# Eight chained sub-layers for four batches on one core: a new service order for each engine's interleaved streams of steps

## The reference, cut to what matters

```python
x = x + tanh(g_xattn[l]) * XATTN[l](layernorm(x), ctx, fside)
x = x + tanh(g_ffn[l])   * FFN[l](layernorm(x))
# 0: XATTN state-space scan over 256 positions (16 states, conv4, softplus, silu gate)
#    FFN   8 experts, top 2, width 176, and a shared expert of width 352
# 1: XATTN two int8 "smooth quant" linears;  FFN ternary SwiGLU, width 1024
# 2: XATTN 16 heads with rms-normalised q, k against ctx; FFN BitNet (int8 rows, ternary weights)
# 3: XATTN one head against ctx;             FFN group-ternary SwiGLU with rms norm
```

## Time and profile before

| | |
|---|---|
| median of 3 runs | 1079.76 us (1079.28 to 1082.18) |
| the profiled execution's own time | 1082.69 us |
| its span, first to last instruction | 1080.9 us |
| mean granted clock of TensorE, of full speed | 0.89 |
| busy: TensorE, VectorE, ScalarE, GpSimd | 856.8, 737.9, 531.3, 274.2 us |

### The profile page before, as it was taken

The page is one execution under the profiler, slowest core; times in us unless marked ns, Lnnn a source line. Parts: engine busy times, 40 slices in busy tenths (PEclk is TensorE's granted clock), DMA queues, the critical chain, the costliest instruction groups (busy, mean ns, idle before and its releaser), DMA issues.

```text
span 1080.9 us, 13019 instructions
## 1 busy us (share of the span) xinstructions
PE 856.8 (79%) x4024; PEld 630.9 (58%) x4024; DVE 737.9 (68%) x1800; ACT 531.3 (49%) x1250; POOL 274.2 (25%) x362
## 2 busy tenths in 40 slices
PE   3365599865899887997987899989998689798465
PEld 1121366544678666665776676669866558476244
DVE  4799967784456997887669888854587743354632
ACT  7654643422563554665533555753454445464313
POOL 1200131102133114431642143406100514100205
PEclk9666689987999999897999999989999989699557
DMA  7622455523433202330542133206211324110002
GB/s 260 196 97 80 134 158 175 167 85 84 133 114 118 59 20 60 103 126 15 141 137 64 50 93 109 63 13 191 85 44 50 88 59 119 43 39 21 15 0 69
DMA packets 46627, 99.39 MB, mean 92 GB/s; under 512 B 4952, under 2 KB 16608, under 8 KB 45408
## 3 DMA queue, kind: packets, MB, share of 16 engines
q1 hardware_dynamic: 37344, 73.40, 21.8%
q0 software_dynamic: 9216, 25.17, 8.4%
HBM read 89.12 MB, written 9.44 MB: 91 GB/s over the span
## 4 chain that ended last, share of the span: by engine, by line
PE 37%; DVE 31%; issue 15%; POOL 9%; ACT 6%; SPq 1%; DMA 0%; POOLq 0%; DVEq 0%; ACTq 0%
PE bk L1260 24%; PE bk L1334 5%; DVE ssm_u L1866 4%; PE bk L1572 2%; DVE ssm_u L1860 2%; PE bk L1541 2%; POOL arA L846 2%; DVE lnbuf L1771 1%; DVE mx L2084 1%; ACT arB L1145 1%; POOL lnbuf L800 1%; DVE arB L2097 1%; POOL aclA L866 1%; PE bk L1684 1%; PE bk L1327 1%
## 5 line engine op out<-in xcount | busy, mean ns | idle before, releaser
L1260 PE MATMUL bk<-hTA,ringT 128*128 128x256 f32 x448 | 115.4, 405 | 1.5 <-DMA ringT<-in_w 0.8
L800 POOL TENSOR_TENSOR lnbuf<-lnbuf,mhalf 128x2 f32<-128x2 f32 x32 | 26.2, 818 | 356.0 <-DVE lnbuf L1777 356.0
L1260 PEld LDWEIGHTS bk<-hTA,ringT 128*128 128x128 f32 x448 | 89.9, 205 | 18.4 <-issue 2.1
L1145 ACT ACTIVATE arB<-bk,nb,rqs 128x256 f32<-128x256 f32 x128 | 70.9, 560 | 30.9 <-DVE nb L2087 30.7
L1866 DVE TENSOR_TENSOR_SCAN ssm_u<-ssm_da,ssm_u 128x512 f32<-128x512 f32 x64 | 81.0, 1265 | 4.7 <-DVE ssm_u L1860 0.5
L1260 PE MATMUL bk<-qk 128*128 128x256 f32 x288 | 79.6, 403 | 5.3 <-ACT arB L1145 2.9
L1260 PE MATMUL bk<-arB,cx 128*128 128x256 f32 x256 | 70.8, 400 | 9.4 <-DVE qk L2132 8.3
L1896 DVE SCALAR_TENSOR_TENSOR t1A<-thA,bk 128x256 f32<-128x256 f32 x88 | 36.6, 416 | 53.9 <-ACT thA L1070 53.5
L1185 ACT ACTIVATE arB<-bk 128x512 f32<-128x512 f32 x64 | 38.2, 596 | 61.9 <-PE bk L1541 61.7
L1334 PE MATMUL bk<-ringM,arB 128*128 128x256 f32 x256 | 66.6, 382 | 1.4 <-ACT arB L1194 1.4
L1063 ACT ACTIVATE ssm_da<-sdl,nega 128x255 f32<-128x255 f32 x128 | 57.0, 501 | 20.5 <-DVE ssm_u L1866 20.0
(11 more groups left out here) (333 smaller groups left out, 2212.9 us busy)
## 6 DMA issues: line engine op xcount, KB each, us to landing
ringT<-in_w SPq DMA_DIRECT2D x56, 384.0 KB, 3.1
ringQ<-in_wqk SPq DMA_DIRECT2D x40, 384.0 KB, 3.1
ring<-q3s POOLq DMA_DIRECT2D x32, 384.0 KB, 3.5
ring<-q7s POOLq DMA_DIRECT2D x32, 384.0 KB, 3.6
ringM<-m4s SPq DMA_DIRECT2D x32, 256.0 KB, 2.6
q3s<-qk SPq DMA_DIRECT2D x4, 512.0 KB, 7.6
q7s<-qk SPq DMA_DIRECT2D x4, 512.0 KB, 4.0
qk<-in_wo SPq DMA_DIRECT2D x4, 512.0 KB, 4.3
```

Of the source, the lines that this page charges most:

```text
L800: g.tensor_tensor(lnr, lnv, mhalf[:, 0:2], ALU.pow).then_inc(*sig(f"{k}.pool", "lnr"))
L1145: s.activation(pm[:, t, :], bank[:, t * S:t * S + S], ACT.Exp, bias=nb4[:, n, t:t + 1], scale=scale(t), accum_out=den4[:, n, t:t + 1]).the ...
L1260: return t_.matmul(dst, lhsT, rhs, start=start, stop=stop)
```

## The change

Only the numbers of `PLAN` change, for all five streams and all parts; some knots are added or dropped. Every step, operation, tile, DMA, wait and signal is the same. What differs is the order in which each engine comes to them. A few of the lines (the tables of the scan states, chunks, heads and rings change in the same way and are left out):

```diff
             "pe": {
-                "group": {0: ((0.15, 586.51), (0.9, 588.82), (2.4, 592.73), (16.15, 614.12), (18.4, 639.13), (32.15, 718.06), (34.4, 768.37),)},
...
-                "h1": {0: ((2.5, 639.64), (4.5, 680.25), (11.5, 798.78),),
...
-                "kp": {0: ((0, 1100.60), (1.5, 1100.61), (2, 1182.86), (3, 1240.57), (4, 1243.48), (5, 1261.89), (6, 1261.90), (6.5, 1263.46), (8.5, 1264.57),)},
...
-                "vo": {0: ((0, 902.41), (1, 902.72), (2, 973.33), (3, 1014.14), (4, 1066.80), (5, 1066.91), (7, 1082.33),)},
...
+                "group": {0: ((0.15, 463.90), (0.9, 463.91), (1.65, 487.73), (2.4, 542.94), (16.15, 700.84), (16.9, 705.75), (17.65, 721.62), (18.4, 722.23), (32.15, 781.82), (32.9, 781.83), (34.4, 783.04),)},
...
+                "h1": {0: ((2.5, 269.52), (11.5, 594.89),),
...
+                "kp": {0: ((0, 1016.60), (1, 1019.71), (1.5, 1020.12), (2, 1191.76), (2.5, 1191.77), (3, 1195.20), (3.5, 1197.41), (4, 1198.00), (5.5, 1202.06), (6.5, 1212.15), (7.5, 1213.26), (8.5, 1213.27),)},
...
+                "vo": {0: ((0, 829.01), (1, 868.45), (2, 876.92), (4, 898.67), (5, 902.38), (6, 997.23), (7, 1014.44),)},
...
             "dve": {
-                "group": {0: ((0.15, 584.93), (4.5, 588.79), (7.5, 626.91), (10.5, 627.22), (16.15, 633.37), (18.4, 639.42), (20.5, 656.13), (22, 658.14), (25, 702.58), (32.15, 773.64), (32.9, 773.65), (33.65, 775.66), (36.5, 776.94), (38, 828.97), (42.5, 831.18),)},
...
-                "h1": {0: ((0, 201.52), (2, 635.65), (5.5, 735.99), (8.5, 752.60), (9.5, 761.71), (10.5, 761.72),),
...
+                "group": {0: ((0.15, 464.31), (1.65, 467.22), (2.4, 535.90), (4.5, 536.21), (6, 542.49), (7.5, 542.50), (10.5, 548.39), (16.15, 722.32), (16.9, 722.33), (17.65, 725.91), (20.5, 729.60), (22, 729.81), (23.5, 731.92), (26.5, 762.23), (32.9, 787.86), (33.65, 804.98), (34.4, 806.97), (36.5, 809.29), (38, 813.75), (42.5, 822.96),)},
...
+                "h1": {0: ((0, 547.11), (9.5, 560.80), (10.5, 601.95),),
...
             "sp": {
-                "vo": {0: ((-1, 708.60), (1, 890.90), (3, 927.60), (5, 1068.37), (8, 1094.36), (9, 1096.46),)},
...
+                "vo": {0: ((-1, 837.07), (1, 868.97), (3, 890.81), (5, 894.42), (8, 1105.43), (9, 1225.71),)},
...
```

More of the change, by code:

```diff
@@ new lines, in build @@
+                "h1": {0: ((2.5, 269.52), (11.5, 594.89),),
+                    1: ((2.5, 1211.73), (11.5, 1214.26),),
+                    2: ((2.5, 2020.45), (11.5, 2030.93),),
+                    3: ((2.5, 2263.97), (4.5, 2264.92), (11.5, 2283.91),)},
+                "head": {0: ((-0.25, 1450.52), (0, 1464.23), (0.39, 1464.24), (1, 1471.53), (1.25, 1472.74), (1.39, 1477.47), (1.64, 1484.95), (2.42, 1484.96), (2.64, 1527.97), (3, 1646.90), (3.42, 1657.83), (3.64, 1657.84), (4.42, 1658.85), (4.64, 1663.75), (5, 1663.76), (5.25, 1667.20), (6, 1671.14), (6.42, 1672.72), (6.64, 1673.58), (7.39, 1675.07), (7.64, 1677.86), (8, 1677.87), (9.42, 1683.81), (9.64, 1690.67), (11.39, 1695.96), (11.64, 1710.97), (12, 1712.38), (12.25, 1712.69), (13.42, 1728.70), (13.64, 1742.59), (14.42, 1742.60), (14.64, 1748.27), (15.42, 1749.65), (17.42, 1777.19),),
[40 rows of a table added]
@@ new lines, in build @@
+                "state": {0: ((-1.2, 203.13), (-0.2, 251.04), (0.8, 311.45), (1.8, 317.33), (3.95, 325.34), (4.8, 359.44), (5.95, 359.75), (6.8, 411.02), (8.95, 432.43), (9.8, 434.44), (13.95, 466.73), (14.95, 537.86), (15.95, 546.57), (16, 546.58),),
[3 rows of a table added]
+                "ternary": {0: ((0.4, 17.54), (1.4, 173.05), (2.4, 215.17), (3.4, 316.22), (4.4, 358.85), (5.4, 413.81),)},
+                "vo": {0: ((0, 829.01), (1, 868.45), (2, 876.92), (4, 898.67), (5, 902.38), (6, 997.23), (7, 1014.44),)},
@@ L405, in build @@
-                "head": {0: ((-0.14, 1824.78), (0.25, 1827.29), (0.44, 1829.99), (1.25, 1832.63), (1.44, 1838.47), (1.81, 1838.48), (2.25, 1843.60), (2.44, 1843.61), (2.81, 1847.26), (3.25, 1858.05), (3.81, 1858.06), (4.25, 1859.83), (6.44, 1871.19), (6.81, 1872.01), (7.25, 1873.02), (7.81, 1878.10), (8.25, 1878.11), (8.81, 1880.46), (9.25, 1880.77), (11.44, 1890.71), (11.81, 1896.88), (12.44, 1898.30), (12.81, 1901.07), (14.44, 1908.79), (14.81, 1912.67), (15.25, 1912.68), (15.81, 1913.09), (18, 1926.01),),
[39 rows of a table removed]
@@ L445, in build @@
-                "state": {0: ((0, 187.39), (0.2, 188.50), (3.7, 223.26), (4, 223.27), (4.2, 225.61), (5, 225.62), (5.2, 236.16), (8, 245.36), (8.2, 379.62), (13.2, 543.80), (13.7, 584.71), (14.2, 616.78), (14.7, 616.79), (15.2, 616.80), (15.7, 625.36), (16, 627.50), (17, 628.51),),
[3 rows of a table removed]
-                "ternary": {0: ((0.5, 84.94), (0.6, 87.55), (1.5, 104.72), (1.6, 159.13), (2.5, 186.72), (2.6, 187.98), (3.5, 217.34), (3.6, 224.75), (4.5, 225.06), (4.6, 239.05), (5.5, 242.35), (5.6, 378.15), (6, 411.76),)},
@@ new lines, in build @@
+                "head": {0: ((-0.14, 1461.96), (0.25, 1467.07), (0.81, 1469.83), (1.25, 1473.95), (1.44, 1479.83), (1.81, 1516.84), (2.25, 1604.80), (2.44, 1642.99), (2.81, 1647.62), (3.25, 1651.93), (3.44, 1651.94), (3.81, 1660.13), (4.44, 1662.43), (4.81, 1665.34), (5.25, 1665.35), (5.81, 1668.81), (6.25, 1669.82), (6.81, 1674.98), (8.25, 1679.96), (8.81, 1682.16), (9.25, 1686.17), (9.81, 1691.88), (10.25, 1691.89), (11.25, 1693.24), (11.44, 1695.25), (11.81, 1700.54), (12.25, 1700.55), (12.81, 1701.81), (13.25, 1741.37), (15.81, 1753.07), (18, 1778.46),),
[39 rows of a table added]
@@ new lines, in build @@
+                "state": {0: ((0, 28.57), (0.2, 201.62), (1.2, 204.73), (1.7, 317.47), (4, 325.32), (4.2, 325.43), (6, 346.58), (6.2, 350.49), (9, 358.41), (9.2, 408.22), (9.7, 421.93), (14, 437.44), (14.7, 465.21), (15, 465.22), (15.2, 467.09), (15.7, 520.31), (16, 539.90), (17, 542.70),),
[3 rows of a table added]
+                "ternary": {0: ((0.5, 29.63), (0.6, 158.54), (1.5, 165.89), (1.6, 177.72), (2.5, 187.72), (2.6, 206.96), (3.5, 319.73), (3.6, 325.41), (4.5, 325.50), (4.6, 349.08), (5.5, 356.13), (5.6, 365.21), (6, 427.15),)},
@@ L454, in build @@
+                "w2": {0: ((0, 137.28), (1, 193.19),),
+                    1: ((0, 1268.83), (1, 1435.96),),
+                    2: ((0, 1746.18), (1, 1765.49),),
+                    3: ((0, 2209.89), (1, 2211.80),)},
             },
             "act": {
-                "copy7": {0: ((0, 663.95), (1, 769.09), (2, 833.76),)},
-                "experts": {0: ((0, -244.70), (1, -149.29), (2, -147.28),)},
-                "group": {0: ((-3, 397.25), (0, 618.27), (13, 626.28), (14.5, 633.29), (16, 639.10), (29, 647.11), (30.5, 699.22), (32, 760.73),)},
@@ L504, in build @@
-                "state": {0: ((-1, 186.23), (0, 186.24), (1, 188.45), (2, 213.95), (4, 220.07), (5, 226.58), (6, 275.35), (8, 348.95), (9, 373.56), (11, 375.57), (13, 585.39), (14, 585.40),),
[3 rows of a table removed]
-                "ternary": {0: ((0, 6.66), (1.5, 92.35), (2, 185.92), (2.5, 185.93), (3, 209.04), (3.5, 217.96), (4.5, 220.57), (5, 237.61), (5.5, 308.12),)},
[5 rows of a table removed]
+                "copy7": {0: ((0, 660.05), (1, 782.91), (2, 811.24),)},
+                "experts": {0: ((0, -42.70), (1, -12.09), (2, -12.08),)},
@@ new lines, in build @@
+                "group": {0: ((-3, 429.93), (0, 432.25), (13, 479.26), (14.5, 537.20), (16, 546.68), (29, 553.99), (30.5, 773.21), (32, 790.52),)},
+                "h1": {0: ((3, 544.48), (7.5, 548.10), (11.5, 681.75),),
+                    1: ((3, 1215.42), (7.5, 1219.73), (11.5, 1245.61),),
+                    2: ((3, 2019.53), (7.5, 2027.14), (11.5, 2029.51),),
+                    3: ((3, 2262.84), (7.5, 2267.18), (11.5, 2289.80),)},
+                "head": {0: ((0.35, 1465.43), (1.3, 1467.62), (1.35, 1475.93), (1.72, 1642.29), (2.3, 1660.60), (2.35, 1660.61), (2.72, 1660.72), (3.3, 1664.63), (3.72, 1664.64), (4.3, 1664.65), (4.35, 1664.66), (5.35, 1664.67), (6.35, 1674.99), (6.72, 1677.00), (7.3, 1679.31), (7.35, 1679.42), (7.72, 1681.32), (8.3, 1682.33), (8.72, 1690.32), (9.3, 1691.03), (9.35, 1692.04), (9.72, 1693.05), (10.3, 1693.43), (10.72, 1700.43), (11.3, 1730.44), (12.35, 1730.45), (13.3, 1730.46), (13.35, 1740.13), (14.3, 1747.73), (14.35, 1747.84), (14.72, 1749.91), (15.3, 1758.12), (15.35, 1758.13), (16.3, 1758.14), (16.72, 1779.22),),
[40 rows of a table added]
@@ new lines, in build @@
+                "state": {0: ((-1, 186.78), (0, 266.09), (1, 266.10), (2, 321.11), (3, 323.48), (4, 324.39), (5, 345.44), (6, 345.45), (7, 347.30), (8, 395.78), (9, 428.89), (10, 429.20), (12, 429.81), (13, 430.94), (14, 431.95),),
[3 rows of a table added]
+                "ternary": {0: ((0, 29.55), (0.5, 70.27), (1, 167.66), (1.5, 175.85), (2, 186.48), (2.5, 191.35), (3, 308.36), (3.5, 322.37), (4.5, 342.61), (5, 348.18), (5.5, 363.08),)},
+                "vo": {0: ((0, 837.97), (1, 872.38), (2, 878.79), (4, 905.17), (5, 936.18), (6, 955.83), (7, 968.94),)},
@@ L514, in build @@
```

(18 more changed lines are left out.)

19 lines of the change are left out of this document (4 added, 15 removed), and 385 rows, old and new, of the table PLAN.

## The result

The changed kernel takes 1074.80 us (median of 5 runs, 1070.27 to 1075.33) for 1080.69 before: ratio 0.9937, 95% interval 0.9917 to 0.9958. In a second measurement it took 1072.10 for 1080.42 (0.9906, 0.9881 to 0.9930). It is faster, by 5.9 and by 8.3 us between the medians; the forecast was 1069.8, its range 1056 to 1087 and its likeliest case holds both medians.

A forecast was written before the change was run, and what follows sets the result against it. Neither TensorE nor VectorE is full; hand-overs that no other batch covers set the time. 1082.7 - 10 (head) - 2 (middle) + 2 (batch 3's start) = 1072.7 us profiled, 1069.8 against the median; range 1056 to 1087.

The forecast's parts named there:

- Step 1: Head: batch 0's routing put right behind `h1` on VectorE ends near 114, 7.6 us earlier.
- Step 2: Head: group work moved behind batch 1's last conv step; 14.6 us of VectorE work leaves, 11.5 taken as gained.
- Step 3: Fewer fillers before the last expert chunk: 8 us less; `s1` of batch 0 added 14 us earlier, bounds 10 and 17.
- Step 4: Within `s2` of batch 0: returning fillers make its hops wait, +4 us, bounds 0 and 18.5.
- case A: The forecast itself, whole kernel: 1058 to 1076.4 us, chance 0.54.
- Rival C: `s2`'s hops each blocked by a whole filler, 18.5 us in place of 4: slower, 1084.3 us; chance 0.24.
- Step 5: Middle: batch 2's earlier `h1` and later first chunk save idle time in the stretch at 487, -2 us.
- Rival B: Head gains 10 us, but the full middle takes 8 back: 1078 to 1080 us; chance 0.16.
- Step 6: Batch 3's start: batch 2's `s5` and `s6` work goes ahead of its first query steps, +2 us, bounds 0 and 6.3.
- Step 8: Tail: TensorE's order is unchanged from place 889 on, so the stretch 929 to 1080.9 stays 151.90 us.

The follow-up runs named there:

- k0_in_s3: `head_new` with batch 0's 16 key fillers moved from between `s2`'s hops into `s3` of batch 0: 1077.68 us (0.9962).
- head_new: The new order up to the first transpose of `s3` of batch 0, the kernel before's old order behind it: 1070.20 us (0.9888).

## Why the prediction was right, and where not

1. *Steps 1 and 2 (routing, group work).* Logits near 109: 107.4. Routing ends near 114: 113.4. Chunk 2 near 128: 127.5. `su` near 122: 121.2. The sizes are right; their shares are not. Step 1 gave 7.6 us to the routing, which alone costs 5; it overlooked that VectorE, once it has no foreign work there, waits 3.45 for the logits. Step 2, the moved group work, is what is left to pay, though it wasn't moved alone. Step 2 also misread a row: the 1.28 us of L1736 in the earlier trace rows are for two evictions, so four take 2.7 and not 5.1, and the work that leaves is 12.1 us and not 14.6. With its allowance for waits cut from the too large figure, 11.5 came out near the 12.4 measured; that is luck, the more as 3.5 of the 12.4 are there at the layer norm already (103.16 for 106.61).
2. *Step 3 (fewer fillers ahead of the last chunk).* `s1` added near 196: 197.8 in the usual run, 193.85 in the fastest, both within 10 to 17 earlier (12.5 and 16.5). Its 8 fillers at 0.86 weren't tried alone.
3. *Step 4 (+4 within `s2`) failed as told.* The size was right (-12.5 becomes -8.3, 4.2 us; from `s1`'s addition to batch 1's first chunk 69.4 for the 69 of case A) and the cause wrong, so the size was luck: fillers between `s2`'s hops cost nothing on balance, since most of that stretch is VectorE's work, and the 4.2 arise behind `s2` (36.7 for 36.8 in `s2`, 32.9 for 28.7 in `s3`), where batch 1's routing went ahead of `s3`'s norm and the last fillers ahead of its transpose. That move was in the order that I read, and step 4 booked it as a gain ("give back"). Rival C had blocked hops as its only mechanism, at 1.6 us and more each, and `k0_in_s3` excludes that within `s2`; in front of `s3`'s first product the fillers do block, by 1.4 us (`k0_in_s3` beside `head_new`). The Trainium skill, "TensorE: Matmul & The Clock Gate", section "HAM oscillation — how this bites in real kernels", says that waits between short bursts bring the clock down. The trace agrees, 0.77 without fillers and 0.91 with them, and shows what the clock was worth in `s2`: 0.57 us in one hop.
4. *Step 5 (middle, -2).* The stretch at 487 has a clock of 0.87 for 0.79, but it is no longer the same work: batch 2's first chunk comes at 509.46 for 496.86, and its 8 matmuls take 2.91 us for 3.76, so the slow matmuls aren't gone as forecast. Between `s3` of batch 0 and `s7` of batch 2 the changed kernel gains nothing and loses 2.3 (-8.3 to -6.0), less than the 6 that the prediction named as its limit, and in the chains much more each way. Rival B (gain given back) describes the middle chain, which was 8.3 ahead and is 2.2 behind at `s3` of batch 1; its price on the whole is 2 to 5 us by the medians over `head_new`, and not 8.
5. *Step 6 (end, +2).* Alone 4 by the medians and 5.7 by the trace, within its bounds of 0 and 6.3; the sum used the low part. Within the new order it isn't a cost at all, and no experiment split that saving further.
6. *Step 8 (tail).* 149.9 for 151.9, taken as unchanged. TensorE's order is the same from place 889 on, but at the time of `s7`'s addition batch 3's own steps are further on.

So the sum of -10 comes out near the measured -6 and -8 by a head whose size was right, and by luck behind it: the middle lost 2.3 where 2 were to be gained, and from `s7` of batch 2 on 2.3 were gained where step 6 had 2 lost.

## What to carry to other kernels

A step that is moved forward on an in-order engine brings its own wait with it; ask what filled that wait before, and what will now. Judge a filler by the engine that the hops wait for, not by the idle time of the engine that it runs on. A hand-made order holds for the lateness of the chains that it was made with: test a new part of it together with what follows, since here the same old end cost nothing behind the old middle and 7 us or more behind the new one.
